# A decoder of two layers in one program: keys in 128+128+1, X loaded in parts, variances aggregated inside the stages, routing inside the dense experts

## What is computed

```python
x = x + _L0_xattn_ref(_layernorm(x), ctx, ctx, ctx)      # gelu(x.ctx) * (x.ctx) . ctx
x = x + _L0_attn_ref(_layernorm(x), ...)                 # linear attention, 16 heads of 64
x = x + _L0_ffn_ref(_layernorm(x), ...)                  # ln1, attention over the batches, proj, ln2, top 2 of 8 experts
x = x + _L1_xattn_ref(_layernorm(x), ctx, ctx, mask, pad_mask, Wq, Wk, Wv, Wo)
x = x + _L1_attn_ref(_layernorm(x), ...)                 # clamped attention, 16 heads, 8 for keys
x = x + _L1_ffn_ref(_layernorm(x), ...)                  # shared expert and top 1 of 8

# _L1_xattn_ref, 16 heads of 8, per batch: 32 queries, 257 keys
qh = apply_rope(heads(q @ Wq.T)); kh = apply_rope(heads(k @ Wk.T)); vh = heads(v @ Wv.T)
scores = einsum('bhqd,bhkd->bhqk', qh, kh) / sqrt(8) + attn_mask
attn = softmax(where(key_padding_mask, -1e9, scores))
out = (attn @ vh, heads merged) @ Wo.T

# _L0_ffn_ref: h1 = hidden + proj(attention(ln1(hidden))), x = ln2(h1)
top_p, top_i = top_k(softmax(x @ router_weight), 2); top_p = top_p / sum(top_p)
# an expert takes at most 1280 rows, in order of row; later ones are dropped
h1 + sum over the two experts of top_p * (gelu(x @ w1[e]) @ w2[e])
```

## Time and profile before

| | before |
|---|---|
| median of 3 runs (lowest, highest) | 2471.78 us (2469.35, 2474.32) |
| the profiled execution | 2464.36 us, its span 2462.7 us |
| granted TensorE clock, mean | 0.95 |
| busy: TensorE, its weight loads, VectorE, ScalarE, GpSimd | 91%, 69%, 64%, 54%, 41% |
| instructions | 90206 |

### The profile page before, as it was taken

How to read it: one execution, slowest core, us unless ns; L and a number is a source line. 1 busy time by engine, 2 the same in 40 slices (tenths; PEclk the granted TensorE clock), 3 DMA queues, 4 the chain that set the end, 5 groups by cost and what they waited for, 6 DMA issues and landing times. The chain is left out here.

```text
span 2462.7 us, 90206 instructions
## 1 busy us (share of the span) xinstructions
PE 2248.3 (91%) x32612; PEld 1707.5 (69%) x32613; DVE 1585.3 (64%) x4583; ACT 1336.3 (54%) x3729; POOL 1020.0 (41%) x924
## 2 busy tenths in 40 slices
PE   5989999987999879997999999999979999979994
PEld 3657777764888757775777777777756656666892
DVE  4567777764877543335777777777756766654442
ACT  3555555556777443333777777777755555542331
POOL 0023333322777400003555555555516666634115
PEclk9999999997999669998999999999989999989997
DMA  5630000000000000000111110111131000000112
GB/s 139 174 123 2 0 0 0 0 1 1 0 0 0 0 1 1 0 0 25 35 33 32 32 32 32 32 32 32 52 127 35 0 0 0 0 1 32 41 43 73
DMA packets 38094, 71.62 MB, mean 29 GB/s; under 512 B 6128, under 2 KB 26480, under 8 KB 37360
## 3 DMA queue, kind: packets, MB, share of 16 engines
q1 hardware_dynamic: 34672, 63.55, 8.5%
q0 software_dynamic: 3328, 6.82, 0.9%
HBM read 60.91 MB, written 9.44 MB: 29 GB/s over the span
## 5 line engine op out<-in xcount | busy, mean ns | idle before, releaser
L2297 DVE CUSTOM_DVE_ANT_0 xat_scores<-bank,xat_mask_b 128x257 f32<-128x257 f32 x512 | 212.5, 423 | 96.8 <-PE bank L2016 90.5
L2169 ACT ACTIVATE xat_scores<-xat_scores,xat_least 128x257 f32<-128x257 f32 x512 | 257.4, 503 | 12.1 <-DVE xat_least L2297 12.1
L2073 PE MATMUL bank<-ident,xat_scores 128*86 128x128 f32 x1536 | 240.4, 280 | 0.0
L2073 PEld LDWEIGHTS bank<-ident,xat_scores 128*86 128x86 f32 x1536 | 157.7, 122 | 83.5 <-ACT xat_scores L2169 40.9
L982 POOL TENSOR_TENSOR gqa_rnorm<-gqa_norm_min,gqa_minus_half 128x12 f32<-128x12 f32 x64 | 145.9, 2279 | 103.7 <-DVE gqa_norm_min L1059 103.7
L2183 ACT ACTIVATE xat_p_T<-bank 86x384 f32<-86x384 f32 x256 | 122.7, 480 | 121.8 <-PE bank L2073 121.8
L629 POOL TENSOR_TENSOR lin_q_softmax<-lin_q_exp,lin_q_rsum 128x512 f32<-128x512 f32 x64 | 66.8, 1043 | 246.0 <-DVE lin_q_rsum L685 246.0
L1599 DVE SCALAR_TENSOR_TENSOR X<-bank,expert_shares,X 128x128 f32 (+1 forms) x256 | 72.0, 343 | 149.0 <-PE bank L1564 149.0
L1585 ACT ACTIVATE moe_gelu<-bank 128x512 f32<-128x512 f32 x128 | 76.5, 597 | 145.7 <-PE bank L1556 145.7
L1323 POOL TENSOR_TENSOR bat_scores<-bat_scores,bat_max 128x512 f32<-128x512 f32 x128 | 131.9, 1041 | 55.8 <-DVE bat_max L1355 54.1
L1564 PEld LDWEIGHTS bank<-moe_w,moe_gelu 128*128 128x128 f32 x1024 | 124.2, 192 | 30.1 <-issue 18.7
(11 more groups left out here) (295 smaller groups left out, 5989.0 us busy)
## 6 DMA issues: line engine op xcount, KB each, us to landing
glu_ctx_N<-in_ctxN SPq DMA_DIRECT2D x32, 576.0 KB, 4.4
xat_ctx_T<-in_ctxT SPq DMA_DIRECT2D x32, 516.0 KB, 3.5
xat_pad<-in_xat_pad SPq DMA_DIRECT2D x32, 128.5 KB, 3.3
expert_w<-in_glx_w SPq DMA_DIRECT2D x1, 4096.0 KB, 14.4
slot_rows<-gqa_zero_rows SPq DMA_DIRECT2D x1, 2560.0 KB, 11.4
slt_rows<-slot_rows SPq DMA_DIRECT2D x40, 64.0 KB, 1.8
slot_results<-slt_y POOLq DMA_DIRECT2D x40, 64.0 KB, 1.8
moe_w<-in_moe_w SPq DMA_DIRECT2D x2, 1024.0 KB, 5.9
```

The source lines that it names most:

```text
L2073: m = pe.transpose(dst[0:JC, c * P:(c + 1) * P], sx[j % 2][g][:, c * JC:(c + 1) * JC], k.ident[:, :])
L2169: act.activation(sx[j % 2][g][:, 0:J], sx[j % 2][g][:, 0:J], ACT.Exp, bias=mn[j % 2][g][:, 0:1], scale=-1.0, accum_out=sm[j % 2][:, g:g + ...
L2297: dve.tensor_tensor_reduce(sx[j % 2][g][:, 0:J], pS[g][:, 0:J], mb[slot][:, j, :], 1.0, BIG, ALU.add, ALU.min, mn[j % 2][g][:, 0:1]).then_ ...
```

## The change

Five things. (1) **Semaphores** of a large stage are no longer cleared in a block of their own; they stay, and SyncE clears them inside the next large stage. (2) **Variances**: the 32 `bn_aggr` leave the deviation phase. A stage makes those of all but its last one or two tiles ahead of its last adds, and those of the last ones right behind their statistics. The projection makes all 32 at its end, the experts 28 ahead of the last block and 4 behind it. (3) **Start**: no load phase and no first deviation phase. In the gated layer X comes in four parts (4, 8, 10 and 10 tiles) between the first four contexts; VectorE takes the statistics of the parts before tile 0 and in tiles 0 to 2, GpSimd the reciprocal deviation as a power of -0.5; tile 0 transposes its context before x. (4) **Layer 0's feed-forward**: HID is made in the batch attention's steps on ScalarE; the routing's instructions move into the experts' stage, on VectorE ahead of its adds, with ScalarE's exp ahead of the gelus and TensorE's two products after the third expert's; there are four result banks in place of two, and TensorE waits for the shares before the fourth result. (5) **Cross attention**: the keys are 128 + 128 + 1. Transposes, value products and output products go in two parts. For the last key, TensorE spreads its weights (a column of the exps) over 32 rows for each group, into the bank of the values, and once a tile makes its values for 4 batches as 4 columns; ScalarE copies both out. On VectorE `o_mix` adds weights x value of that key to the output, and the multiply by the reciprocal row sum, `o_keep`, goes to GpSimd, with its inputs double-buffered.

```diff
-def clear_semaphores(nc, sems):
-    with nc.Block() as block:
-        @block.sync
-        def _(sp):
-            for s in sems:
-                sp.sem_clear(s)
+def clear_stale(sp, k):
+    for s in k.stale:
+        sp.sem_clear(s)
+def leave_stale(k, sems, scope):
+    k.stale_scope.close()
+    k.stale, k.stale_scope = sems, scope
...
+def aggregate(dve, k, chain, counted, lo, hi):
+    dve.wait_ge(chain, counted)
+    for t in range(lo, hi):
+        dve.bn_aggr(k.MV[:, t, :], k.BNS[:, t, :])
+def residual_tile(dve, k, t, add, chain, done, late=1):
     dve.tensor_tensor(k.X[:, t, :], k.X[:, t, :], add, ALU.add).then_inc(chain, 1)
     wait_apart(dve, chain, done + 1)
     dve.bn_stats(k.BNS[:, t, :], k.X[:, t, :]).then_inc(chain, 1)
+    if isinstance(t, int) and t >= NT - late:
+        aggregate(dve, k, chain, done + 2, t, t + 1)
...
         def _(act):
-            act.wait_ge(mv, NT)
             act.activation(k.SD[:, :], k.MV[:, :, 1], ACT.Sqrt, bias=k.eps[:, 0:1]).then_inc(sq, 1)
...
         def _(dve):
-            for t in range(NT):
-                dve.bn_aggr(k.MV[:, t, :], k.BNS[:, t, :]).then_inc(mv, 1)
             dve.wait_ge(sq, 1)
...
+        GROUPS = ((0, 4), (4, 12), (12, 22), (22, 32))
+        half_neg = sb("minus_half", [P, NT])
...
+            clear_stale(sp, k)
             def load(t, slot):
                 sp.dma_start(cN[slot][:, :, :, :], ctxN[t]).then_inc(landed[slot], 16)
-            for t in range(WAYS):
+            sp.dma_start(k.ident[:, :], ident).then_inc(ident_landed, 16)
+            x_rows = x.rearrange("(t b) s h -> (b s) t h", b=BT)
+            for t, (lo, hi) in enumerate(GROUPS):
+                sp.dma_start(k.X[:, lo:hi, :], x_rows[:, lo:hi, :]).then_inc(x_landed[t], 16)
                 load(t, t)
...
                 if isinstance(t, int) and t == 0:
-                    transpose(t, slot)
+                    pe.wait_ge(ident_landed, 16)
                     for b in range(BT):
                         ctx_transpose(t, slot, b)
+                    transpose(t, slot)
...
+            def look_at(g):
+                lo, hi = GROUPS[g]
+                dve.wait_ge(x_landed[g], 16)
+                for t in range(lo, hi):
+                    dve.bn_stats(k.BNS[:, t, :], k.X[:, t, :]).then_inc(stats, 1)
+                dve.wait_ge(stats, hi)
+                for t in range(lo, hi):
+                    dve.bn_aggr(k.MV[:, t, :], k.BNS[:, t, :]).then_inc(means, 1)
             def norm(t, slot):
+                if isinstance(t, int) and t in (0, 4):
+                    dve.wait_ge(rstd_done, 1 if t == 0 else len(GROUPS))
...
+                    look_at(1)
                     gate(t, slot)
+                if isinstance(t, int) and 1 <= t < 3:
+                    look_at(t + 1)
...
+                if isinstance(t, int) and t == NT - 1:
+                    aggregate(dve, k, added, 2 * t, 0, t)
...
+            look_at(0)
             tiles(dve, body)
+        @block.gpsimd
+        def _(pool):
+            pool.memset(half_neg[:, :], -0.5).then_inc(set_up, 1)
+            pool.wait_ge(set_up, 1)
+            for g, (lo, hi) in enumerate(GROUPS):
+                pool.wait_ge(means, hi)
+                pool.tensor_scalar(k.SD[:, lo:hi], k.MV[:, lo:hi, 1], 1.0, EPS, ALU.mult, ALU.add).then_inc(var_eps, 1)
+                pool.wait_ge(var_eps, g + 1)
+                pool.tensor_tensor(k.RSTD[:, lo:hi], k.SD[:, lo:hi], half_neg[:, lo:hi], ALU.pow).then_inc(rstd_done, 1)
...
-                if hidden:
-                    act.activation(k.HID[:, t, :], src[:, t, :], ACT.Identity, bias=k.SHIFT[:, t:t + 1],
-                                   scale=k.RSTD[:, t:t + 1]).then_inc(kept, 1)
...
+            def keep_row(t):
+                act.activation(k.HID[:, t, :], k.X[:, t, :], ACT.Identity, bias=k.SHIFT[:, ts(t, 1)],
+                               scale=k.RSTD[:, ts(t, 1)]).then_inc(kept, 1)
...
                 t_copy(s, 0)
+                keep_row(s)
...
+            def ranks():
+                pe.wait_ge(ones_set, 1)
+                pe.wait_ge(sel_ready, 1)
+                pe.matmul(pR, low[:, :], sel[:, :, :], start=True, stop=True)
+                pe.matmul(pC, ones[:, :], sel[:, :, :], start=True, stop=True).then_inc(ranked, 1)
...
+            def y(n, e):
+                pe.wait_ge(gelued, NF * n + NF)
+                wait(pe, added, TB * (n - WAYS + 1))
+                if isinstance(n, int) and n == WAYS - 1:
+                    pe.wait_ge(known, 1)
...
+            def body(b, first, last):
+                for e in range(E):
+                    h(b, e)
+                    if e or not first:
+                        y(E * b + e - 1, (e - 1) % E)
+                    if first and e == 2:
+                        ranks()
...
+            dve.tensor_tensor(k.COMB[:, :, 0:E], pr[:, :, :], tmp[:, :, :], ALU.mult).then_inc(known, 1)
+            dve.wait_ge(known, 1)
...
+    NC, LAST = 2, J - 1
...
-                for c in range(NJ):
+                for c in range(NC):
                     for g in range(G):
                         r = slice(32 * g, 32 * g + 32)
                         m = pe.matmul(dst[r, OC], va[j % 2][:, c, r], pt[j % 2][g][:, c * P:(c + 1) * P],
-                                      start=(c == 0), stop=(c == NJ - 1))
+                                      start=(c == 0), stop=(c == NC - 1))
                 m.then_inc(no_made, 1)
             def v(t, slot, j, at):
                 dst = unit_bank(*at)
-                for c in range(NJ):
-                    m = pe.matmul(dst[0:JC, c * P:(c + 1) * P], cT[slot][:, j, c * JC:(c + 1) * JC], wv[:, :],
-                                  start=True, stop=True)
+                if j == 0:
+                    pe.matmul(dst[:, LC], wv[:, :], cT[slot][:, :, LAST], start=True, stop=True)
+                for c in range(NC):
+                    pe.matmul(dst[:, c * P:(c + 1) * P], cT[slot][:, j, c * P:(c + 1) * P], wv[:, :],
+                              start=True, stop=True)
+                for g in range(G):
+                    m = pe.matmul(dst[32 * g:32 * g + 32, PC], sx[j % 2][g][:, LAST:J].broadcast_to([P, 32]),
+                                  k.ident[:, :], start=True, stop=True)
                 m.then_inc(v_made, 1)
...
                     if some:
                         if j == 1:
-                            wait(pe, o_kept, u - 2)
+                            wait(pe, o_mixed, u - 2)
...
                     if j == 1 and not last:
-                        wait(pe, o_kept, u - 1)
+                        wait(pe, o_mixed, u - 1)
                         x_transpose(t + 1, 1 - slot, (j, XX))
                     if j == 2 and not last:
-                        wait(pe, o_kept, u - 1)
+                        wait(pe, o_mixed, u - 1)
                         q(t + 1, 1 - slot, (j, XX))
                     if j == 3 and not first:
-                        pe.wait_ge(o_kept, u - 1)
+                        pe.wait_ge(o_mixed, u - 1)
                         y(t - 1, 1 - slot, (j, XX))
...
+                wait(act, o_mixed, u - 1)
+                if j == 0:
+                    act.activation(vl[slot][:, :], unit_bank(*at)[:, LC], ACT.Copy).then_inc(vl_copied, 1)
+                act.activation(va[j % 2][:, :, :], unit_bank(*at)[:, 0:PC.stop].rearrange("p (c f) -> p c f", f=P),
                                ACT.Copy).then_inc(v_copied, 1)
...
+            def o_keep(t, slot, j):
+                u = BT * t + j
+                pool.wait_ge(o_mixed, u + 1)
+                pool.wait_ge(n_copied, u + 1)
+                wait(pool, y_made, t - 1)
+                pool.tensor_tensor(os_[slot][:, :, j, :], om[j % 2][:, :, :], nb[j % 2][:, :, :],
+                                   ALU.mult).then_inc(o_kept, 1)
+            def read_pad(t, slot):
                 pool.wait_ge(pad_landed[slot], 16 * (half(t, slot) + 1))
...
+                if not first:
+                    o_keep(t - 1, 1 - slot, 2)
+                if not last:
+                    read_pad(t + 1, 1 - slot)
+                if not first:
+                    o_keep(t - 1, 1 - slot, 3)
                 if not last:
                     keep_mask(t + 1, 1 - slot)
+                o_keep(t, slot, 0)
+                if not last:
+                    keep_ctx(t + 1, 1 - slot)
                     add_mask(t + 1, 1 - slot)
-                    keep_ctx(t + 1, 1 - slot)
                     rotate_q(t + 1)
+                o_keep(t, slot, 1)
+                if not last:
                     spread_q(t + 1, 1 - slot)
+                if last:
+                    o_keep(t, slot, 2)
+                    o_keep(t, slot, 3)
...
-            def o_keep(t, slot, j, at):
-                dve.wait_ge(n_copied, BT * t + j + 1)
-                wait(dve, y_made, t - 1)
-                dve.tensor_tensor(os_[slot][:, :, j, :], unit_bank(*at)[:, OC].rearrange("p (h q) -> p h q", q=S),
```

(11 more changed lines are left out.)

277 lines of the change are left out of this document (128 added, 149 removed).

## The result

| | before | after |
|---|---|---|
| median (lowest, highest) | 2470.57 us of 4 runs (2468.89, 2474.32) | 2440.61 us of 4 runs (2432.15, 2441.20) |
| the profiled execution, its span | 2464.36, 2462.7 us | 2432.15, 2430.4 us |
| granted TensorE clock, mean | 0.950 | 0.962 |

The ratio is 0.9873 (95% interval 0.9854 to 0.9892): 30 us less, where 13 were forecast. The profiled execution of after lies 8 us under its median, that of before 6 us; the other three runs of after lie within 1 us of each other. By the profiled executions the kernel got 32 us shorter.

A forecast was written before the change was run, and what follows sets the result against it. Cross attention, the longest stage, was taken as bound by TensorE and VectorE's loop nearly equally, then by GpSimd's order; start -11, borders -8, norm -11.6, routing -15.6, cross attention +33 gave -13, median 2459 us, range 2425 to 2502.

The follow-up runs named there:

- e6: The kernel after with GpSimd's cross-attention list reordered: spread_q ahead of o_keep(t,1), add_mask behind o_keep(t-1,3); 2391.14 us, ratio 0.9700 to the kernel before.

## What to carry to other kernels

Work given to an engine with slack is priced by its place in that engine's order, not by its length: with one order of GpSimd's list the stage is 19 us longer than before, with another 32 us shorter (e6). Before a pause of TensorE is called harmless or costly, work out its length from both sides, when it is ready and when it is released; here half a microsecond more of it a tile cost 54 us. And when a stage's length changes though its steps don't, look at when the clock falls at its end.
